# A two-layer attention and expert kernel: rows summed on TensorE, one weight transfer per tile, expert loads spread out

## What is computed

```python
x = x + _L0_xattn_ref(_layernorm(x), ctx_2048, ctx_2048, ...)      # 16 heads
x = x + _L0_ffn_ref(_layernorm(x), gate_w, w13, w2)                # 64 experts, 8 chosen
x = x + _L1_xattn_ref(_layernorm(x), ctx_2048, ctx_2048)
x = x + _L1_ffn_ref(_layernorm(x), router_w, expert_bias, ...)     # 16 experts, 4 chosen

def _L1_xattn_ref(q, k, v):
    scaled = jnp.einsum('bsd,bse->bde', q, k) * scale
    attn = jax.nn.softmax(scaled, axis=1)
    return jnp.einsum('bde,bse->bsd', attn, v)
```

## Time and profile before

| | us |
|---|---|
| median of three runs | 764.34 |
| lowest and highest | 762.84, 764.79 |
| the profiled execution | 764.58 |
| its span | 762.8 |

### The profile page before, as it was taken

How to read it: one execution, slowest core, us unless ns; L and a number is a source line. 1 busy time by engine, 2 the same in 40 slices (tenths; PEclk the granted TensorE clock), 3 DMA queues, 4 the chain that set the end, 5 groups by cost and what they waited for, 6 DMA issues and landing times.

```text
span 762.8 us, 12322 instructions
## 1 busy us (share of the span) xinstructions
PE 506.1 (66%) x3519; PEld 377.7 (50%) x3519; DVE 378.6 (50%) x1235; ACT 224.9 (29%) x578; POOL 351.0 (46%) x476
## 2 busy tenths in 40 slices
PE   1725986878867323998879951677618878777760
PEld 1611543434432113977668840555517767666750
DVE  8955555877773530443334425888522222222226
ACT  0550353555555101332223311344302111211210
POOL 9483111445544550554455460144465545455530
PEclk9975888998996655999999975677859999999995
DMA  5199997644665796799974328611247767787837
GB/s 166 45 191 309 310 279 212 176 153 135 204 206 184 256 416 191 235 341 323 302 263 165 92 93 306 270 56 63 78 145 227 247 225 252 227 249 248 282 128 275
DMA packets 88291, 162.57 MB, mean 213 GB/s; under 512 B 13742, under 2 KB 58814, under 8 KB 86448
## 3 DMA queue, kind: packets, MB, share of 16 engines
q1 hardware_dynamic: 62208, 104.83, 43.1%
q0 software_dynamic: 13968, 32.29, 11.6%
q10 hardware_dynamic: 12064, 24.84, 11.1%
HBM read 103.56 MB, written 66.78 MB: 223 GB/s over the span
## 4 chain that ended last, share of the span: by engine, by line
PE 17%; DMA 14%; issue 12%; SPq 8%; DVE 5%; POOL 1%; another core or an unknown queue 1%; POOLq 1%; ACT 1%; DVEq 1%
DMA hd_side<-held 5%; PE hd_ps_up L1216 5%; DMA listed<-sc_empty,sc_index 2%; DMA sc_tile_rows<-listed 2%; PE hd_ps_out L1222 2%; DMA rows<-hd_side_out,hd_side_target 2%; SPq L426 2%; SPq L424 2%; DMA sc_rows<-rows 2%; PE sc_ps L1697 2%; PE hd_ps_x L1194 1%; PE sc_ps L1759 1%; SPq L1604 1%; PE sc_ps L1709 1%
## 5 line engine op out<-in xcount | busy, mean ns | idle before, releaser
L990 DVE TENSOR_REDUCE at_top<-at_ps_top 128x2 f32<-128x512 f32 x128 | 83.3, 683 | 59.6 <-PE at_ps_top L901 54.3
L1363 POOL DMA_INDIRECT rows<-hd_out,hd_rows x64 | 62.4, 975 | 72.9 <-DVE hd_out L1314 45.9
L1062 ACT ACTIVATE at_prob<-at_ps_score 128x512 f32<-128x512 f32 x128 | 72.3, 594 | 53.7 <-PE at_ps_score L919 42.4
L1759 PEld LDWEIGHTS sc_ps<-sc_t_turned,e_up_w 128*112 128x112 f32 x672 | 82.2, 183 | 5.7 <-issue 3.0
L1216 PE MATMUL hd_ps_up<-hd_x_turned,e_arena 128*128 128x160 f32 x512 | 84.9, 310 | 0.0
L1759 PE MATMUL sc_ps<-sc_t_turned,e_up_w 128*112 128x128 f32 x672 | 83.6, 279 | 1.9 <-DMA e_down_w<-in_down 1.8
L1216 PEld LDWEIGHTS hd_ps_up<-hd_x_turned,e_arena 128*128 128x128 f32 x512 | 78.3, 197 | 8.9 <-issue 6.2
L685 POOL DMA_INDIRECT held<-e_extended,e_address x64 | 63.1, 986 | 33.7 <-issue 18.9
L901 PE MATMUL at_ps_top<-e_arena 96*128 96x256 bf16 x256 | 58.0, 316 | 25.2 <-PEq L107 21.3
L1660 POOL DMA_INDIRECT rows<-sc_out,sc_target x42 | 41.3, 982 | 67.9 <-DVE sc_out L1903 61.7
L1351 DVE TENSOR_TENSOR hd_inner<-hd_silu,hd_ps_up 128x160 f32<-128x160 f32 x64 | 20.6, 321 | 92.1 <-ACT hd_silu L1301 62.0
(11 more groups left out here) (266 smaller groups left out, 930.5 us busy)
## 6 DMA issues: line engine op xcount, KB each, us to landing
e_arena<-in_weights SPq DMA_DIRECT2D x52, 384.0 KB
e_up_w<-in_up SPq DMA_DIRECT2D x42, 448.0 KB
held<-e_empty ACTq DMA_DIRECT2D x16, 960.0 KB, 5.7
hd_rows<-held SPq DMA_DIRECT2D x15, 768.0 KB
e_down_w<-in_down SPq DMA_DIRECT2D x42, 224.0 KB
sc_rows<-rows SPq DMA_DIRECT2D x8, 1024.0 KB, 13.7
sc_tile_rows<-listed SPq DMA_DIRECT2D x42, 144.0 KB
parts<-op_parts SPq DMA_DIRECT2D x8, 576.0 KB
```

Source lines behind the costliest of these rows:

```text
L990: nc.vector.reduce_max(top[:, 2 * h:2 * h + 2], ps_top[at % TOPS][:], AX_X).then_inc(top_found, 1)
L1062: nc.scalar.activation(prob[at % RING][:], ps_score[at % SCORES][:], ACT.Exp, scale=scale).then_inc(prob_ready, 1)
L1363: nc.gpsimd.indirect_dma_start(rows_out, to, out_ap, None, bounds_check=TOKENS * LAYER0.chosen - 1, oob_is_err=False).then_inc(semaphore, 16)
L1759: op = nc.tensor.matmul(ps_up[u % 2][:, part, c * P:(c + 1) * P], up_w[u][:, k, at:at + W], t_turned[u % 2][:, k, :], start=k == 0, stop=k ...
```

## The change

There are four parts.

1. In the held stage the expert loads go out three per group (`AGAIN`), in groups 0 to 10.
2. In the feature stage `add_rows` is one halving of 1024 columns on VectorE. TensorE's new `sum_rows(b)` adds the four rows left and x with five float32 matmuls by the identity into PSUM, and VectorE and ScalarE read the sum there. `sum_rows(t + 2)` stands at the end of TensorE's step t, behind `attend(t)`. `bring_x` and `keep_warm` go. A third PSUM bank holds x.
3. In the expert stage up and down weights of an expert lie in one array padded to 128 partitions (704 KB an expert, with zero entries past the last expert), and one DMA loads them. The expert is the column shifted right, so SP reads one register per tile, ahead of its wait. The first six columns are read before the first loads.
4. `pick` goes ahead of VectorE's wait for silu, with a wait for the tile's rows.

```diff
 class Experts:
-        self.up = [s.sbuf(f"up_w{u}", [P, 2, 2 * layer.inter], F32) for u in U]
-        self.down = [s.sbuf(f"down_w{u}", [layer.width, layer.chunks, D], F32) for u in U]
+        self.w = [s.sbuf(f"w{u}", [P, down_at + layer.chunks * D], F32) for u in U]
...
-    def load(self, sp, i, u):
-        at = bass.ds(i * self.layer.unroll + u, 1)
-        e = sp.value_load(self.tile_expert[0:1, at], min_val=0, max_val=self.layer.experts - 1)
-        for to, of in self.transfers:
-            sp.dma_start(to[u][:], of[bass.ds(e, 1)].rearrange("a p k n -> (a p) k n")).then_inc(self.loaded[u], 16)
+    def column(self, engine, i, u):
+        at = bass.ds(i * self.layer.unroll + u, 1)
+        return engine.value_load(self.tile_column[0:1, at], min_val=0, max_val=self.layer.columns + 2 * self.layer.unroll - 1)
+    def load(self, sp, column, u):
+        e = column >> (self.layer.lists.bit_length() - 1)
+        sp.dma_start(self.w[u][:], self.weights_dram[bass.ds(e, 1)].rearrange("a p n -> (a p) n")).then_inc(self.loaded[u], 16)
 def held_phase:
-                for e in range(EACH * g, EACH * (g + 1)):
-                    if e + ring.SLOTS < E:
-                        ring.load(sp, e + ring.SLOTS)
+                for e in range(ring.SLOTS + AGAIN * g, min(ring.SLOTS + AGAIN * (g + 1), E)):
+                    ring.load(sp, e)
 def second_phase, SP:
             last = groups(sp)
+            columns = [experts.column(sp, 0, u) for u in range(U)]
             for u in range(2):
-                experts.load(sp, 0, u)
+                experts.load(sp, columns[u], u)
...
                 for u in range(U):
+                    c = experts.column(sp, i, u)
                     sp.wait_ge(inner_ready, i * U + u - U + 1)
                     sp.sem_inc(sp_parted, 1)
-                    load_tile(i, u)
+                    load_tile(i, u, c)
                     sp.wait_ge(down_done, i * U + u - U + 1)
                     sp.sem_inc(sp_parted, 1)
-                    experts.load(sp, i, u)
+                    experts.load(sp, c, u)
 second_phase, TensorE:
-            def bring_x(b):
+            def sum_rows(b):
                 pe.wait_ge(added, b + 1)
-                if b >= 2:
-                    pe.wait_ge(x_kept, b - 1)
-                nc.tensor.matmul(ps_x[b % 2], consts.identity[:], rows[b][:, 0, :], start=True, stop=True)
+                if b >= 3:
+                    pe.wait_ge(x_kept, b - 2)
+                for k in range(HALF):
+                    nc.tensor.matmul(ps_x[b % 3], consts.identity[:], rows[b][:, k, :], start=k == 0, stop=False)
+                nc.tensor.matmul(ps_x[b % 3], consts.identity[:], x_all[:, b, :], start=False, stop=True).then_inc(summed, 1)
...
+            sum_rows(0)
             for t in STEPS:
                 if 1 <= t <= B:
-                    keep_warm()
                     routing.pe_turn(pe, t - 1)
-                if 0 <= t < B:
-                    bring_x(t)
...
                     attend(t)
+                if t + 2 < B:
+                    sum_rows(t + 2)
 second_phase, VectorE:
             def add_rows(b):
                 dve.wait_ge(rows_loaded[b], 16)
-                width = HALF
-                while width >= 1:
-                    link(nc.vector.tensor_tensor(rows[b][:, 0:width, :], rows[b][:, 0:width, :], rows[b][:, width:2 * width, :], ALU.add))
-                    width //= 2
-                nc.vector.tensor_tensor(rows[b][:, 0, :], rows[b][:, 0, :], x_all[:, b, :], ALU.add).then_inc(added, 1)
+                nc.vector.tensor_tensor(rows[b][:, 0:HALF, :], rows[b][:, 0:HALF, :], rows[b][:, HALF:, :], ALU.add).then_inc(added, 1)
...
                 if first:
-                    dve.wait_ge(added, t + 2)
-                    norms.dve_stats(link, 0, rows[t + 1][:, 0, :])
+                    dve.wait_ge(summed, t + 2)
+                    norms.dve_stats(link, 0, ps_x[(t + 1) % 3])
...
 def pick:
+                dve.wait_ge(tile_loaded[u], i * 16 + 16)
 def step:
+                pick(i, u, free)
                 dve.wait_ge(silu_done, i * U + u + 1)
-                pick(i, u, free)
```

More of the change, by code:

```diff
@@ L1571, in second_phase @@
         banks = [s.psum(f"ps{n}", [P, 2 * D]) for n in range(8)]
-        ps_x = [banks[n][:, 0:D] for n in range(2)]
+        ps_x = [banks[n][:, 0:D] for n in (0, 1, 7)]
         ps_scores = banks[2][:].rearrange("p (c n) -> p c n", c=2)
@@ L1583, in second_phase @@
         rows_loaded = [s.sem(f"rows_loaded{b}") for b in range(B)]
-        added, normed, scored, top_known, expo_ready, share_ready, vals_ready, attended, x_kept = (
-            s.sem(n) for n in ("added", "normed", "scored", "top_known", "expo_ready", "share_ready", "vals_ready", "attended", "x_kept"))
+        added, summed, normed, scored, top_known, expo_ready, share_ready, vals_ready, attended, x_kept = (
+            s.sem(n) for n in ("added", "summed", "normed", "scored", "top_known", "expo_ready", "share_ready", "vals_ready", "attended", "x_kept"))
         cleared = [s.sem(f"cleared{u}") for u in range(U)]
@@ L1602, in _, with load_tile @@
         def _(sp):
-            def load_tile(i, u):
-                c = sp.value_load(experts.tile_column[0:1, bass.ds(i * U + u, 1)], min_val=0, max_val=layer.columns + 2 * U - 1)
+            def load_tile(i, u, c):
                 sp.wait_ge(cleared[u], i * 16 + 16)
@@ L1708, in attend @@
                 for c in range(2):
-                    op = nc.tensor.matmul(ps_x[b % 2], vals_shared[b % 2][:, c, :], expo[b % 2][:, c, :], start=False, stop=c == 1,
+                    op = nc.tensor.matmul(ps_x[b % 3], vals_shared[b % 2][:, c, :], expo[b % 2][:, c, :], start=False, stop=c == 1,
                                           skip_group_check=True)
                 op.then_inc(attended, 1)
-            def keep_warm():
-                for _ in range(WARM_UP):
-                    nc.tensor.matmul(ps_t[0][:, 0, :], consts.earlier[:], consts.ones[:], start=True, stop=True)
-            pe.wait_ge(joined.first_layer_done, 1)
+            sum_rows(0)
             for t in STEPS:
                 if 1 <= t <= B:
-                    keep_warm()
                     routing.pe_turn(pe, t - 1)
-                if 0 <= t < B:
-                    bring_x(t)
                 if 1 <= t <= B:
@@ L1753, in up @@
                 pe.wait_ge(turned_kept, i * U + u + 1)
-                pe.wait_ge(weights_loaded[u], (i + 1) * (16 * len(experts.transfers)))
+                pe.wait_ge(weights_loaded[u], i * 16 + 16)
                 for part in range(2):
@@ L1800, in _ @@
                         act.wait_ge(scored, t)
-                    norms.act_apply(act, t, 0, x_norm[(t + 1) % 2][:], rows[t + 1][:, 0, :], normed)
+                    norms.act_apply(act, t, 0, x_norm[(t + 1) % 2][:], ps_x[(t + 1) % 3], normed)
                 if 1 <= t <= B:
@@ L1922, in _ @@
                 link(nc.vector.tensor_tensor(rows[b][:, 0, :], rows[b][:, 0, :], rows[b][:, 1, :], ALU.add))
-                nc.vector.tensor_tensor(x_all[:, b, :], rows[b][:, 0, :], x_all[:, b, :], ALU.add).then_inc(last_summed, 1)
+                nc.vector.tensor_tensor(x_all[:, b, :], rows[b][:, 0, :], x_all[:, b, :], ALU.add).then_inc(added, 1)
 def two_layers(nc, x, ctx, ctx_turned, consts_f, more, weights, biases, rotary, merge_weights,
                merge_biases, gate0, weights0,
-               gate1, gate1_bias, up1, down1, out):
+               gate1, gate1_bias, weights1, out):
     def scratch(name, shape, dtype=F32):
@@ L1989, in gates @@
         return w.T.reshape(2, P, -1).transpose(1, 0, 2)
+    E1, W1, UP1 = LAYER1.experts, LAYER1.width, 4 * LAYER1.inter
+    past = (LAYER1.columns + 2 * LAYER1.unroll - 1) // LAYER1.lists + 2
+    weights1 = np.zeros((past, P, UP1 + LAYER1.chunks * D), np.float32)
     up1 = np.concatenate([L1_ffn_gate_proj, L1_ffn_up_proj], axis=2)
+    weights1[0:E1, :, 0:UP1] = up1.reshape(E1, 2, P, -1).transpose(0, 2, 1, 3).reshape(E1, P, UP1)
+    weights1[0:E1, 0:W1, UP1:] = L1_ffn_down_proj.reshape(E1, LAYER1.chunks, W1, D).transpose(0, 2, 1, 3).reshape(E1, W1, -1)
     return {
```

33 lines of the change are left out of this document (15 added, 18 removed).

## The result

The changed kernel takes 771.73 us (median; 767.01 to 773.89) against 765.5 for the one before on the same chip (762.22 to 769.66): ratio 1.0075, 95% interval [1.0046, 1.0104]; the pairs in brackets below are such intervals too. The change makes the kernel a little slower. The forecast was 753.5 us and faster, with a range of 740 to 769. The profiled execution of the changed kernel has a span of 768.9 us.

What follows compares the result with a forecast made beforehand. Bounds were taken as transfers (held stage), a ring of three engines (feature stage) and SP's issuing (experts); 762.8 - 7 + 21 - 22 - 3 = 751.8, plus 1.8 outside the span, given as 753.5 us, range 740 to 769.

Steps and rivals of the forecast that it cites:

- Held stage: Held stage: three loads a group cut the transfer volume, groups come 8.88 us apart instead of 10.12, -7 us.
- What leaves VectorE: Feature stage: VectorE's adds shrink by 1.6 us a step but lie beside the critical chain, gain 0.
- What TensorE gets: Feature stage: statistics wait for attend and the sum, 2.6 us late in each of seven steps, 18 us.
- The 0.6 taken off: Feature stage: 0.2 us for dropped `bring_x` and 0.4 for sometimes fast scores, lowering a step's delay from 3.2 to 2.6.
- the part ahead of the first maximum: Feature stage, batch 0: its sum stands ahead of everything, 4.25 us in place of 1.6, partly covered, +2 us.
- that behind the last: Feature stage, last three steps: without sum or `keep_warm` TensorE falls to 1.2 GHz, +1 us.
- the clock stays low: Feature stage rival: without `keep_warm` the clock falls in each gap and rises only after the sum, +38 us; chance 0.15.
- the forecast +21: Feature stage as a whole: the late sums, batch 0 and the last three steps together cost 21 us.
- Expert stage: Expert stage: SP's issue stops being the bound, a tile takes 3.4 us instead of 4.02, -22 us.
- The start: Start of the expert stage: first six column reads made before the scatter wait, so loads follow earlier, -3 us.
- the 2.6 us for a late sum: Feature stage: delay of each step from statistics awaiting the sum, with one of five sum matmuls at the low clock.
- the 3.4 us a tile from transfers as the next bound: Expert stage: transfers and TensorE, both near 3.0 us a tile, overlap imperfectly at a 0.92 share, making 3.4.

Runs made afterwards that it cites:

- e9: Changed kernel with each sum issued one step earlier and batches 0 to 2 added fully on VectorE; 743.5 us, ratio 0.9765 to the kernel before.
- e10: Changed kernel without the sums on TensorE, feature stage as before the change; 741.08 us, ratio 0.9718 to the kernel before.
- e6: Changed kernel with 56 small bfloat16 warm-up matmuls on constants put back ahead of each turn; ratio 1.0019 to the kernel before.
- e13: Changed kernel with two weight transfers a tile, a second register read and the column read behind the product wait; ratio 1.0238 to the kernel before.
- e14: Changed kernel with only the read of a tile's column moved back behind the wait for the product; ratio 1.0085 to the kernel before.
- e11: Changed kernel with the 36 weight loads after the first six tiles left out; one run, experts 139.2 us against 142.9 in the changed kernel.
- e7: Changed kernel with the expert stage's loops over groups written out on every engine; ratio 1.0026 to the kernel before.

## Why the prediction was wrong

**Held stage: right.** 8.73 us a group against 8.88 forecast, -8.1 us over all runs against -7. Volume over the measured rate was the right sum.

**What leaves VectorE: right.** In the changed kernel taking the adds off was worth nothing. The halving takes 1.21 us, and later VectorE idles 1.69 us ahead of the logits; with the sums early (e9) the steps add up to the same as with all adds on VectorE (e10).

**What TensorE gets: the mechanism right, the size wrong.** The statistics wait behind attend and sum, nothing of it is hidden, and seven steps pay. Forecast was 1.91 + 0.85 + 4 x 0.43 - 1.29 = 3.2 and then 0.6 off, 2.6 us a step; measured 3.93. Three terms:
- The sum takes 2.72 + 0.45 = 3.17 us instead of 2.57, +0.6. I let the clock rise after one of five matmuls, since it had risen about there before. Now about 1.4 more of the five run at 1.2 GHz (0.6 / 0.42). That the warm-up matmuls had helped it up before is likely by e6, where the first four take 1.89 us in three steps, but e6 has 56 of them and the kernel before 24.
- From TensorE's end to the statistics 0.12 us pass (510.40 to 510.52), which I had left out.
- The 0.6 taken off, for `bring_x` and for key scores that are sometimes fast, came in no step: from the statistics to the next maximum it is 8.55 us against 8.51. With the sum ending 4.5 us ahead of the turn, TensorE is back at 1.2 GHz: 0.69 us for each turn but one (0.44), and 1.89 for the key scores.

3.2 + 0.6 + 0.1 = 3.9. Over seven steps that is 27.9 us (63.92 to 91.85) where I had 18; the part ahead of the first maximum gave +2.0 as forecast, that behind the last +3.5 where I had +1.

The rival "the clock stays low" was half right, which a forecast of separate cases had no place for: the clock fell in the gaps, as it said, and rose in the middle of each sum and not behind it. By its own figures it meant +38, the forecast +21, and the stage got +33. I had written what speaks for it, 4.4 us of idle where there had been 2.25, and gave it 0.15 because the sum is a longer dense stretch. That stretch ends ahead of the gap, and the clock it had won was lost again behind 4.5 us of idle. What the Trainium skill, "TensorE: Matmul & The Clock Gate", section "Why this matters for your kernels", says there, that idle gaps between bursts bring the half rate back, agrees with this trace: 4.5 us idle, then 1.89 us for key scores, two matmuls like attend's, which takes 0.96 at 2.4 GHz.

**Expert stage: the direction right, the next bound wrong.** SP dropped out as the bound, as SP's waits in the changed kernel and e13 against e14 show. The start gave -3.6 (first six tiles, 20.0 to 16.4 us) where I had -3. A tile takes 3.61 us and not 3.4. I took transfers near their limit as what comes next, at a share of 0.92; the share is 0.83, and without the weight transfers (e11) a tile still takes 3.52. In free stretches a tile takes 2.83 us (turns at 615.27 and 618.10). The rest, 0.78 us a tile or 27 us in 35, goes with the pauses; that they are all of it is my reading of the traces, since no run is without them. They stood in the trace of before, from 611 to 741 us, and I had no term for them:

```profile
ACT sc_silu L1826 <- remote: 36.7, 8, 5.9
```

The 17 us of error are so mainly the step's 1.4 us x 7 = 10, with 2.5 behind the last maximum, and the experts' 0.2 us x 35 = 7. Two steps of the prediction failed: the 2.6 us for a late sum, which let the clock rise too early and took 0.6 off for gains that didn't come (3.93 measured), and the 3.4 us a tile from transfers as the next bound (3.61 measured, and not set by the weight transfers). The held stage was 2.7 us better than forecast in this trace, so it made the error smaller by luck.

## What to carry to other kernels

Work moved to an engine with free time can still cost its full length, if another engine reads its result before doing anything else. Ask at which place of the ring it is awaited, and put it one step earlier (8.9 us a step instead of 13.7 for the same work). Where warm-up work is removed, price everything behind the next gap at the low clock, in every step, and take nothing off for a rate that the removed work had bought. And when a bound falls, look in the old trace for idle time that nothing explains, before taking the next busiest resource as the new bound.

## What the runs showed of the hardware

- ScalarE pauses some 4 to 8 us with its data ready, about five to ten times in 36 tiles: with loops or without (e7), at a transfer share of 0.83 or 0.27 (e11), in the kernel before too. In the 38 idle stretches of ScalarE counted above, GpSimd never rested longer than 1.1 us; the cause is open. TensorE has slow stretches as well, in which single matmuls come 0.7 us apart with nothing to wait for; the changed kernel, TensorE in time, at the end of a pause of ScalarE (628.02 to 635.80):

```profile
634.14 0.27 PE L1752 MATMUL sc_ps<-sc_t_turned,e_w 128*112 128x128 f32 x1 [1.16 <-issue]
634.85 0.27 PE L1752 MATMUL sc_ps<-sc_t_turned,e_w 128*112 128x128 f32 x1 [0.45 <-issue]
```

- Splitting a 704 KB transfer in two costs the transfers nothing that shows. It counts on the queue that issues them: two transfers, a second read and a late read together cost 11.8 us in 42 tiles (e13), singly at most 4.1.
- The clock recovered inside one float32 sum of five matmuls (2.72 us for the first four, between the 3.4 and 1.7 of the two levels) and was lost again in the 4.5 us of idle behind it, in five of the first six steps with a turn (0.69 us; the sixth took 0.44).
